# Attention's software pipeline carried one head deeper, with a third score buffer and a fixed split of the first count

## The reference, cut to what matters

```
dots = einsum('bhij,hk->bkij', q k^T * scale, pre_proj)      # 16 heads, 16 memory keys + 512 tokens
dots = where(causal, neg, dots)
vk = lax.top_k(dots, 64)[0][..., -1:]                        # the 64th largest of each query
attn = softmax(where(dots < vk, neg, dots))
attn = einsum('bhij,hk->bkij', attn, post_proj)
out = einsum('bhij,bhjd->bhid', attn, v)                     # then the output projection and bias
```

## Time and profile before

| | |
|---|---|
| median of 3 runs | 1031.14 us (1031.12 to 1031.69) |
| the profiled execution | 1030.79 us, of which the span from first to last instruction is 1029.1 us |
| busy over the span | PE 88%, DVE 81%, ACT 71%, POOL 47% |
| attention, first to last `spread_scale` | 190.5 to 855.1 us, 64 heads |
| mean granted clock of TensorE | 0.957 of full speed |

### The profile page before, as it was taken

The page is one execution under the profiler, slowest core; times in us unless marked ns, Lnnn a source line. Parts: engine busy times, 40 slices in busy tenths (PEclk is TensorE's granted clock), DMA queues, the critical chain, the costliest instruction groups (busy, mean ns, idle before and its releaser), DMA issues.

```text
span 1029.1 us, 16288 instructions
## 1 busy us (share of the span) xinstructions
PE 903.0 (88%) x4151; PEld 579.7 (56%) x4151; DVE 836.7 (81%) x2931; ACT 727.5 (71%) x1868; POOL 487.2 (47%) x1113
## 2 busy tenths in 40 slices
PE   8866778899999999999999999788899779899998
PEld 4623435566666666666666666566666556433432
DVE  4587994999999899999999999989999884446344
ACT  6332325899999999999999999878999684311211
POOL 2000003677777677767777777556777561000000
PEclk9768989899999999999999999999999899999999
DMA  5865130000000000000000000000000000000000
GB/s 156 151 126 92 60 33 1 2 2 2 2 2 2 2 2 2 2 2 2 1 2 1 2 2 2 2 1 2 1 2 2 1 2 1 1 0 11 11 0 21
DMA packets 15007, 18.16 MB, mean 18 GB/s; under 512 B 2656, under 2 KB 12192, under 8 KB 14240
## 3 DMA queue, kind: packets, MB, share of 16 engines
q1 hardware_dynamic: 14880, 16.85, 7.9%
HBM read 11.08 MB, written 5.77 MB: 16 GB/s over the span
## 4 chain that ended last, share of the span: by engine, by line
PE 28%; DVE 23%; ACT 23%; issue 13%; POOL 6%; POOLq 6%; DVEq 1%; DMA 0%; ACTq 0%
DVE Ex L1121 7%; ACT Ex L761 5%; ACT unread L750 5%; ACT unread L742 4%; DVE Sx L1031 4%; ACT unread L734 3%; ACT turned L769 3%; POOL spread L1362 3%; PE bFGI L456 3%; PE bBC L565 2%; POOLq L1325 2%; PE bA L565 2%; PE bFGI L574 2%; PE bFGI L566 2%; PE bBC L566 2%
## 5 line engine op out<-in xcount | busy, mean ns | idle before, releaser
L1343 POOL TENSOR_TENSOR mixed<-Sx,nthr 128x528 f32<-128x528 f32 (+3 forms) x256 | 186.2, 759 | 11.6 <-issue 11.6
L456 PEld LDWEIGHTS bFGI<-spread,Ex 128*128 128x128 f32 x1280 | 156.3, 199 | 54.2 <-POOL spread L1362 52.5
L456 PE MATMUL bFGI<-spread,Ex 128*128 128x128 f32 x1280 | 161.4, 284 | 18.2 <-POOL spread L1362 18.2
L470 PE MATMUL bH<-turned 128*128 128x512 f32 (+3 forms) x512 | 153.2, 442 | 25.1 <-ACT turned L769 24.7
L742 ACT ACTIVATE unread<-Sx,nthr 128x144 bf16<-128x144 f32 (+3 forms) x256 | 143.9, 563 | 20.1 <-POOL nthr L1324 19.2
L1121 DVE SCALAR_TENSOR_TENSOR Ex<-mixed,yk,Ex 128x144 f32<-128x144 f32 (+3 forms) x256 | 147.2, 627 | 1.7 <-DVE yk L1145 1.0
L750 ACT ACTIVATE unread<-mixed,least 128x528 bf16<-128x528 f32 (+3 forms) x256 | 143.4, 565 | 0.0
L470 PEld LDWEIGHTS bH<-turned 128*128 128x128 f32 x512 | 92.1, 189 | 86.5 <-issue 66.2
L761 ACT ACTIVATE Ex<-Sx,nmax 128x144 f32<-128x144 f32 (+3 forms) x256 | 125.5, 563 | 0.0
L1070 DVE MAX8 top<-mixed 128x8 f32<-128x528 f32 (+3 forms) x256 | 110.7, 492 | 0.0
L1362 POOL TENSOR_TENSOR spread<-ident,rinv 128x512 f32<-128x512 f32 x64 | 66.6, 1040 | 70.5 <-DVE rinv L1124 70.5
(11 more groups left out here) (348 smaller groups left out, 1735.0 us busy)
## 6 DMA issues: line engine op xcount, KB each, us to landing
heads_store<-per_head SPq DMA_DIRECT2D x2, 1152.0 KB, 5.0
mixed<-heads_store SPq DMA_DIRECT2D x16, 144.0 KB, 11.0
mixed_store<-mixed SPq DMA_DIRECT2D x2, 1152.0 KB, 4.2
per_head<-mixed_store SPq DMA_DIRECT2D x16, 144.0 KB, 6.2
xr<-in_xT SPq DMA_DIRECT2D x4, 256.0 KB, 3.5
w_s<-in_w12T SPq DMA_DIRECT2D x1, 1024.0 KB, 14.2
outT<-xc SPq DMA_DIRECT2D x4, 256.0 KB, 2.0
wq_s<-in_WqT SPq DMA_DIRECT2D x1, 512.0 KB, 3.9
```

The lines of the kernel that those rows point to most:

```text
L456: last = mm(bFGI[:, k * P:k * P + P], Ex[g % 2][:, t, a:a + P], spread[:, t, :], start=True, stop=True)
L470: last = mm(bH[:, jt * P:T], u[:, jt, :], PT[:, at:at + n], start=h + jt == 0, stop=False)
L1343: Gp.tensor_tensor(y[ph][t], Sx[ph][:, t, 0:NT[t]], nthr[ph][1][:, t:t + 1].broadcast_to((P, NT[t])), ALU.add).then_inc(sem("y_ready"), 1)
```

## The change

Scores are fetched three heads ahead instead of two, `Sx` and `nmax` have three buffers, and `scores` is split into `scores_wide` (400 and 528 columns) and `scores_narrow` (144 and 272 columns) with `values` between them on PE. DVE fetches the two wide tiles ahead of `read_hits`, the narrow ones behind it. ACT does `count` first in its turn, and `tally` for head g+2. POOL does `shift` first in its turn. The first count of the tiles of 400 and 528 columns is on ACT in all heads; before, the one of 400 columns was on DVE in every second head. To make room, `hsilu`, `decay` and the third `unread` are placed in other buffers. The core of the diff, in the order of the four hunks PE, ACT, DVE, POOL behind the first two:

```diff
-def first_on_vector(g):
-    return 2 + g % 2
+COUNTED_ON_VECTOR = (0, 1)
...
-        Sx = [sb(f"Sx{i}", [P, TT, W]) for i in range(2)]
+        Sx = [sb(f"Sx{i}", [P, TT, W]) for i in range(3)]
...
@@ -585,19 +588,21 @@
+                    projected(g)
                     found(g)
-                    projected(g)
+                if 0 <= g + 4 < HEADS:
+                    scores_wide(g + 4)
                 if 0 <= g - 1:
                     values(g - 1)
...
-                if 0 <= g + 3 < HEADS:
-                    scores(g + 3)
-                if g + 4 < HEADS:
-                    keys(g + 4)
+                if 0 <= g + 4 < HEADS:
+                    scores_narrow(g + 4)
+                if g + 5 < HEADS:
+                    keys(g + 5)
...
@@ -803,32 +808,30 @@
-                if g + 3 < HEADS:
-                    key_copy(g + 3)
-                if 0 < g + 1 < HEADS:
-                    tally(g + 1)
+                if g + 4 < HEADS:
+                    key_copy(g + 4)
+                if 0 <= g + 1 < HEADS:
+                    count(g + 1)
+                if 0 <= g < HEADS:
+                    value_copy(g)
+                if 0 <= g - 1:
+                    turned_copy(g - 1)
+                if 0 <= g + 2 < HEADS:
+                    tally(g + 2)
...
                 if 0 <= g + 1 < HEADS:
                     weigh(g + 1)
...
+                if 0 <= g + 3 < HEADS:
+                    first_tally(g + 3)
...
@@ -1019,41 +1022,41 @@
-                if g + 2 < HEADS:
-                    dve.wait_ge(sem("s_done"), 3 * (g + 2) + 1)
+                if g + 3 < HEADS:
+                    dve.wait_ge(sem("s_done"), 3 * (g + 3) + 3)
...
+                if coming:
+                    free_for_fetch(g + 3)
+                    fetch(g + 3, (2, 3))
+                if there:
                     read_hits(g)
                     pick_tops(g)
                     add_tops(g)
                 if coming:
-                    free_for_fetch(g + 2)
-                    fetch(g + 2, (0,))
+                    fetch(g + 3, (0,))
                 if there:
                     last_kept(g)
                 if coming:
-                    fetch(g + 2, (1, 2))
-                    measure_first(g + 2)
-                    fetch(g + 2, (3,))
+                    fetch(g + 3, (1,))
+                    measure_first(g + 3)
...
@@ -1370,25 +1376,26 @@
                 if 0 <= g + 1 < HEADS:
-                    second_threshold(g + 1)
+                    shift(g + 1)
+                if g >= 0:
+                    pick_last(g)
+                if 0 <= g + 2 < HEADS:
+                    second_threshold(g + 2)
                 if g >= 1:
                     weigh_memory(g - 1)
-                if g >= 0:
-                    pick_last(g)
-                if g + 3 < HEADS:
-                    stage_memory_keys(g + 3)
-                if 0 <= g + 1 < HEADS:
-                    third_threshold(g + 1)
-                    shift(g + 1)
-                if 0 <= g + 2 < HEADS:
-                    first_threshold(g + 2)
+                if g + 4 < HEADS:
+                    stage_memory_keys(g + 4)
+                if 0 <= g + 3 < HEADS:
+                    first_threshold(g + 3)
...
+                if 0 <= g + 2 < HEADS:
+                    third_threshold(g + 2)
                 if g >= 0:
                     spread_scale(g)
```

More of the change, by code:

```diff
@@ L169, in mixed_layers_kernel @@
         over = [sb(f"over{i}", [P, TT]) for i in range(2)]
-        unread = [sb(f"unread{i}", [P, STOT], BF16) for i in range(3)]
+        unread = [sb(f"unread{i}", [P, STOT], BF16) for i in range(2)]
+        unread_last = work[:, :, :].rearrange("p t n -> p (t n)")[:, 0:STOT]
         away = sb("away", [P, TT])
@@ L184, in mixed_layers_kernel @@
         rmax = [sb(f"rmax{i}", [P, TT]) for i in range(2)]
-        nmax = [sb(f"nmax{i}", [P, TT]) for i in range(2)]
+        nmax = [sb(f"nmax{i}", [P, TT]) for i in range(3)]
         rsum = sb("rsum", [P, TT])
@@ L438, in scores, with scores_narrow @@
                     pe.wait_ge(sem("fetched"), TT * (g - 1) + 2)
[L439 to L449, removed]
+                mm(scores_in[2], xn[:, b, 2 * P:3 * P], k[:, 0:NT[2]], start=True, stop=True)
+                mm(scores_in[3][:, 0:MEM], xn[:, b, 3 * P:4 * P], k[:, 0:MEM], start=True, stop=True).then_inc(sem("s_done"), 1)
+                mm(scores_in[3][:, MEM:W], xn[:, b, 3 * P:4 * P], k[:, MEM:W], start=True, stop=True).then_inc(sem("s_done"), 1)
+            def scores_narrow(g):
+                b, h = divmod(g, H)
+                k = Y[g % 2]
+                if g:
+                    pe.wait_ge(sem("fetched"), TT * g)
+                for t in range(2):
+                    last = mm(scores_in[t], xn[:, b, t * P:t * P + P], k[:, 0:NT[t]], start=True, stop=True)
+                last.then_inc(sem("s_done"), 1)
             def turn_weights(g):
@@ L515, in _ @@
                     keys(0)
-                    scores(0)
+                    scores_wide(0)
+                    scores_narrow(0)
                     keys(1)
@@ L575, in down4 @@
                 last.then_inc(sem("mo_down"), 1)
-            for g in range(-2, HEADS + 1):
+            for g in range(-3, HEADS + 1):
                 if g == 1:
@@ L732, in first_tally @@
                 act.wait_ge(sem("thr0_ready"), g + 1)
-                for t in range(first_on_vector(g), TT):
-                    last = nc.scalar.activation(unread[1][:, OFF[t]:OFF[t] + NT[t]], Sx[g % 2][:, t, 0:NT[t]], ACT.Sign, bias=cf[g % 2][:, 0, t:t + 1],
+                for t in (t for t in range(TT) if t not in COUNTED_ON_VECTOR):
+                    last = nc.scalar.activation(unread[1][:, OFF[t]:OFF[t] + NT[t]], Sx[g % 3][:, t, 0:NT[t]], ACT.Sign, bias=cf[g % 2][:, 0, t:t + 1],
                                                 accum_out=above[:, t:t + 1])
@@ L1047, in tally @@
                 dve.wait_ge(sem("thr0_ready"), g + 1)
-                for t in range(first_on_vector(g)):
-                    last = V.tensor_scalar(unread[1][:, OFF[t]:OFF[t] + NT[t]], Sx[g % 2][:, t, 0:NT[t]], cf[g % 2][:, 0, t:t + 1], 0.0, ALU.is_ge, ALU.add,
+                for t in COUNTED_ON_VECTOR:
+                    last = V.tensor_scalar(unread[1][:, OFF[t]:OFF[t] + NT[t]], Sx[g % 3][:, t, 0:NT[t]], cf[g % 2][:, 0, t:t + 1], 0.0, ALU.is_ge, ALU.add,
                                            accum_out=above[:, t:t + 1])
@@ L1145, in last_kept @@
                 V.tensor_tensor(yk[:, :].bitcast(I32), vk_p.bitcast(I32), flips[:, :], ALU.bitwise_xor).then_inc(sem("yk_ready"), 1)
-            for g in range(-2, HEADS):
-                there, coming = 0 <= g, g + 2 < HEADS
+            for g in range(-3, HEADS):
+                there, coming = 0 <= g, g + 3 < HEADS
                 if g == 0:
+                    dve.wait_ge(sem("s_done"), 3 * (g + 3) + 3)
                     V.tensor_copy(steer_p, steer_s[:, 5, :]).then_inc(sem("steer_moved"), 1)
@@ L1185, in _ @@
                 if coming:
[L1186 to L1187 removed]
+                    tally(g + 3)
+                if g == -3:
                     down_add(B - 1)
```

96 lines of the change are left out of this document (43 added, 53 removed).

## The result

The changed kernel takes 1130.3 us in the median of 4 runs (1129.0 to 1132.9) against 1031.4 us: the ratio is 1.095, interval 1.090 to 1.099. It is slower by about 99 us; 1160 us was forecast, with a range of 1085 to 1185 (the forecast's own range was 1130 to 1190, so the result lies at its lower edge). The profiled execution has a span of 1127.2 us, 98.1 more than before.

A forecast was written before the change was run, and what follows sets the result against it. DVE was taken as nearly full, with POOL's chain its one wait. 60 turns at 12.31 us against 10.21 give +126, last three -1, lead-in +4: 1030.8 + 129 = 1159.8, forecast 1160 us, range 1085 to 1185 (own range 1130 to 1190).

The forecast's parts named there:

- what moves: POOL's shift follows spread at once and meets DVE's near in every head; both take turns, as if laid end to end.
- the lead-in: Before the first flip, one more head to fetch, tally and score; some 4 us (0 to 8) show.
- MAX at R+4.85: DVE's MAX rows start 4.85 us after the start of rinv (R) in place of 2.59, near being held by shift.
- MAX to hits 2.86: On DVE, four MAX 1.66 us, then the two wide fetches 0.50 and 0.70: hits at R+7.71, R being rinv's start.
- Hits to `keep` 1.88 and a stall of 0.62: On DVE, 3.08 us less two fetches, 1.88; then redo_missed's register load, no longer fully covered, shows 0.62 (bounds 0, 0.62).
- `keep` to `rinv` 2.10: End of DVE's turn: 2.1 us without shift beside it, before up to 2.52.
- PE's new wait: DVE's flip waits for the next head's narrow scores, ready at R+12.9 (R: rinv's start); flip comes at R+13.1, covered by 0.2 us.
- PE's path from the wide scores to the narrow ones: On PE, wide scores 1.91 us, values 2.39, narrow scores 0.87, together 5.2 us.
- Near goes ahead: Rival, 13%: DVE's near waits only for shift's first tile, then POOL waits; a turn of 11.1 us, 1088 us.
- No hold-up: Rival, 7%: near isn't held, POOL's chain sets the hits at R+5.75 (R: rinv's start); turn 10.35 us, 1042 us.
- The change does what it should: Rival, 12%: near isn't held, the register load is covered, ACT's 9.99 us a turn is the bound; 1021 us.
- Worse: Rival, 6%: a turn over 13 us, from PE's lower clock, or all near held with keep still 2.52 us (1213 us).

The follow-up runs named there:

- reordered: Changed kernel with POOL's shift late, ACT's order turned (copy, tally, value_copy, count), PE's found ahead of projected and narrow scores directly behind wide: 1031.5 us, ratio 1.002.

## Why the prediction was right

**The cause, and the side it came out on.** The step "what moves" held: `shift` follows `spread` at R+1.26, `near` starts at R+1.36, and they take turns tile by tile. It is shown in two ways that don't rest on each other: `near` in a form that isn't held runs at its own length and lets `shift` do so, and the place of `shift`, with late `shift` giving `near` its 1.3 us back and early `shift`, as the one edit, costing 90 us.

**The size.** The sum had +126 for 60 turns, -1 for the last three, +4 for the lead-in. The spans show 92.1 for the first 60 turns after the first `rinv` (727.3 us against 635.2), +1.3 for the last three, +3.9 for the lead-in (`rinv` of head 0 at 194.14 against 190.26) and +0.8 behind attention: 98.1. So the term that was too large is the turn, +1.54 us on average instead of +2.10. Its parts, as forecast and in the first head shown above:

- MAX at R+4.85 (its own terms, 1.30 + 2.92 + 0.76 less 0.1, give 4.88): R+4.50, or R+5.04 in a head where `flip` waits for PE. The two laid end to end overstated the first case by 0.35 us: `near`'s part that goes with the columns was put at 0.76 us, all of it added to `shift`, but `shift` grew by 0.37 us only (3.23 against 2.86 where `near` has the form that isn't held). My reading is that the start-up of a POOL tile runs beside `near`'s columns, as the 540.25 start of the second tile before `near`'s 540.58 end suggests; no run separates it.
- MAX to hits 2.86: 2.76.
- Hits to `keep` 1.88 and a stall of 0.62, together 2.50: 2.32 here and in some 30 of the first 60 heads, 2.01 in the next head and in 25 in all. The stall is there (0.47 us in the head above), but it does not show in full, and in the 25 it is 0.16 us.
- `keep` to `rinv` 2.10: 2.07, with `shift` gone from beside it.

Together 11.65 us where 12.31 was forecast; a head with the wait for PE takes 11.9 or 12.2 us.

**PE's new wait.** "Covered by 0.2 us only" was said of the wait of `flip`, and it did come, in 32 heads, 40 us in all between 270 and 930 us. The experiment without it shows that it costs nothing of its own while `shift` is early: what it delays would be held anyway. The 0.2 us of cover went because the turn came out shorter than forecast (that wait is up to 0.18 us where the clock is full), and in the heads where it is long, to a lower clock, below.

**The rivals.** "Near goes ahead" fell: `near` gives way before every tile, and 1.94 us for the form that isn't held against 3.14 leaves no doubt that it waits. "No hold-up" fell with it. "The change does what it should" fell too, and `reordered`, which keeps the depth and the buffers, says more: even without the hold-up and with PE and ACT in a better order the change only comes out level with before. The edits do not add up. With `shift` early the better order gives little (1121.6 against 1130.3 us, ratios 1.090 and 1.095, intervals that overlap); with `shift` and `count` late and PE's order left, some 34 us are won, by the ratios; with PE's order mended as well, 95. How much of the bound with `shift` late lies in the change's order, and how much in my move of `count`, stays open. "Worse" named something that came, the lower clock, but it cost nothing that a run shows, and the size was wrong.

## What to carry to other kernels

When an instruction is moved on one engine, ask what will run beside it on the engine that was seen to hold it up or to be held by it (here POOL and DVE), and read the price from rows where the two already meet, however short. A VectorE instruction that looks busy may be waiting: compare the same form with and without the neighbour. And count from the event on which both depend: here `rinv` releases both `spread` with `shift` behind it and `flip` with `near` behind it, so they met in every head. Last, a hold-up that is taken away pays only as far as the next bound: moving `shift` back out was worth some 34 us in one order of PE and ACT and 90 in another.

## What the runs showed that I had not expected

PE's clock. In the stretch from the first to the last head a mean of 0.92 was granted where it was 0.99 before. Stretches of the changed kernel:

```profile
542.50:546.00 3.50, 1.04 (x6) 0.54 (x6) 3.47 (x16) 3.50 (x12) 1.74 (x8) 1.00 0.00 0
546.00:549.40 3.40, 3.40 (x8) 1.69 (x7) 2.93 (x14) 3.40 (x11) 1.55 (x4) 0.52 0.01 2
...
552.90:569.80 16.90, 13.21 (x84) 10.16 (x82) 16.39 (x58) 16.22 (x45) 10.73 (x27) 1.00 0.01 2
569.90:573.30 3.40, 3.40 (x6) 1.34 (x7) 3.19 (x16) 2.42 (x6) 1.98 (x5) 0.52 0.00 0
```

and the timeline of PE:

```profile
533.80 0.91 PE L439 MATMUL bBC<-Y,xn 128*128 128x400 f32 x2 [1.48 <-DVE rmax L1034]
...
537.78 0.87 PE L450 MATMUL bA<-Y,xn 128*128 128x144 f32 x4
...
543.64 0.27 PE L479 MATMUL bA<-pick,ones_w 128*1 128x64 f32 x2 [0.93 <-POOL pick L1359]
545.44 0.97 PE L439 MATMUL bBC<-Y,xn 128*128 128x400 f32 x2 [1.53 <-DVE rmax L1034]
...
546.49 2.06 PE L441 MATMUL bBC<-Y,xn 128*128 128x512 f32 x2
...
551.11 0.87 PE L450 MATMUL bA<-Y,xn 128*128 128x144 f32 x4
...
558.52 1.10 PE L441 MATMUL bBC<-Y,xn 128*128 128x512 f32 x2
```

PE, waiting first for the mask and then for the wide fetches, was busy for 1.04 of 3.50 us, no single wait being longer than 1.53 us; in the next 3.40 us 0.52 of the full 2.4 GHz was granted, which is the lower level, 1.2 GHz, for nearly all of it, and the 512-column part of the wide scores took 2.06 us instead of 1.10. Such a stretch comes every 24 us or so, sometimes after 34, and each of the 24 long waits of `flip` for PE (over 1 us) falls in a head behind one. PE's path from the wide scores to the narrow ones, which the prediction put at 5.2 us, takes 6.5 us in such a head (545.44 to 551.98) and 4.9 in the head before (533.80 to 538.65). The lower clock does not cost the time: where DVE no longer waits for PE, at 0.93, the time stays the same (1126.7 us, above). With `shift` late, 0.98 to 0.99 was granted again between 250 and 840 us.

Also unexpected: instructions over four columns, 0.2 us long by themselves, take up to 1.00 us when they are held, so that a tiny instruction ahead of a held one takes over part of its wait.
